# Two-layer ViT tower: the first expert layer's results are added by the scatter DMA in DRAM instead of on VectorE

## The reference

```
h = tok(x)                                        # patches, layer norm, product with W
h = h + quantised_attention(layernorm(h))         # layer 0
h = h + experts_of_4(layernorm(h))                # layer 0: each token goes to ONE of 4 experts (192 -> 768 -> 192)
h = h + linear_attention(layernorm(h))            # layer 1
h = h + experts_of_8(layernorm(h))                # layer 1: each token goes to TWO of 8 experts, weighted sum
```

## Time and profile before

| what | us |
|---|---|
| three runs: median (lowest to highest) | 627.05 (625.25 to 629.93) |
| the profiled execution's own time | 627.9 |
| its span, first to last instruction | 626.1 |
| busy in the span: PE / DVE / ACT / POOL | 503.8 / 326.7 / 206.9 / 143.4 |
| mean granted TensorE clock, share of full | 0.867 |

### The profile page before, as it was taken

One profiled execution on the slowest core, in us unless ns is written; L12 is line 12 of the kernel. 1 busy time (PEld: TensorE's weight loads), 2 busy tenths in 40 slices (PEclk: granted clock), 3 DMA queues, 4 the chain that ended last, 5 costly groups with the idle time before them and its releaser, 6 DMA issues.

```text
span 626.1 us, 12431 instructions
## 1 busy us (share of the span) xinstructions
PE 503.8 (80%) x4338; PEld 462.8 (74%) x4339; DVE 326.7 (52%) x1046; ACT 206.9 (33%) x439; POOL 143.4 (23%) x148
## 2 busy tenths in 40 slices
PE   4999999886543593799999599916999999999960
PEld 4999995465432493689999485915899999999950
DVE  1668999678998786122221464794222222222207
ACT  4620034666993164034343151250222111221110
POOL 1590000000001000533421100004344544343220
PEclk9999999899556575699999787856999999999995
DMA  9981000000004002965669400025866665567116
GB/s 321 409 317 22 1 1 1 1 3 1 0 2 177 2 0 102 227 202 161 187 187 369 136 2 0 1 101 163 243 182 184 201 201 166 162 186 200 55 54 273
DMA packets 35379, 81.41 MB, mean 130 GB/s; under 512 B 7142, under 2 KB 18242, under 8 KB 34306
## 3 DMA queue, kind: packets, MB, share of 16 engines
q1 hardware_dynamic: 29762, 69.37, 33.9%
q0 software_dynamic: 5568, 11.41, 6.5%
HBM read 70.33 MB, written 10.42 MB: 129 GB/s over the span
## 4 chain that ended last, share of the span: by engine, by line
PE 69%; DVE 15%; ACT 6%; DMA 4%; issue 3%; SPq 2%; ACTq 0%; POOL 0%; DVEq 0%; POOLq 0%
PE ps L1088 18%; PE ps L847 14%; PE ps L1064 12%; PE ps L1072 6%; DVE h L1855 2%; PE ps L828 2%; PE ps L827 2%; DMA arena<-ffn_b 2%; PE ps L787 1%; PE ps L959 1%; PE ps L931 1%; DVE xT L1699 1%; PE ps L812 1%; PE ps L932 1%; DVE arena L1567 1%
## 5 line engine op out<-in xcount | busy, mean ns | idle before, releaser
L1088 PE MATMUL ps<-arena,xn 128*128 x696 | 123.3, 328 | 4.1 <-ACT xn L737 1.8
L1088 PEld LDWEIGHTS ps<-arena,xn 128*128 128x128 f32 x696 | 111.8, 190 | 6.6 <-issue 6.4
L481 POOL DMA_INDIRECT xT<-rows,from_i x58 | 56.0, 966 | 189.7 <-DVE from_i L1713 132.7
L1064 PE MATMUL ps<-xn,arena 128*128 128x128 f32 x696 | 91.6, 283 | 3.0 <-DMA arena<-ffn_b 2.0
L847 PE MATMUL ps<-arena 128*128 128x192 f32 (+1 forms) x588 | 86.3, 339 | 9.0 <-ACT arena L520 9.0
L1064 PEld LDWEIGHTS ps<-xn,arena 128*128 128x128 f32 x696 | 88.4, 199 | 4.8 <-DMA arena<-ffn_b 3.1
L847 PEld LDWEIGHTS ps<-arena 128*128 128x128 f32 (+1 forms) x588 | 84.8, 199 | 9.2 <-ACT arena L520 8.7
L494 POOL DMA_INDIRECT made<-xT,to_i x58 | 57.0, 983 | 110.6 <-DVE xT L1750 65.0
L1738 DVE COPY xn<-ps 128x128 f32<-128x128 f32 x58 | 16.9, 292 | 123.6 <-PE ps L1056 104.7
L740 ACT ACTIVATE xn<-ps 128x384 f32<-128x384 f32 x78 | 32.6, 493 | 126.2 <-PE ps L1074 100.1
L737 ACT ACTIVATE xn<-ps,b_all 128x128 f32<-128x128 f32 x114 | 30.9, 389 | 46.8 <-PE ps L1074 35.3
(11 more groups left out here) (368 smaller groups left out, 798.3 us busy)
## 6 DMA issues: line engine op xcount, KB each, us to landing
arena<-ffn_a SPq DMA_DIRECT2D x58, 384.0 KB
arena<-ffn_b SPq DMA_DIRECT2D x116, 96.0 KB
arena<-x_blocks SPq DMA_DIRECT2D x16, 384.0 KB, 6.8
arena<-x_strips SPq DMA_DIRECT2D x3, 1536.0 KB, 12.2
arena<-ffn SPq DMA_DIRECT2D x4, 1152.0 KB, 10.6
rows<-xn SPq DMA_DIRECT2D x8, 384.0 KB, 2.3
arena<-made SPq DMA_DIRECT2D x4, 768.0 KB, 6.7
arena<-tok_w SPq DMA_DIRECT2D x8, 288.0 KB, 7.1
```

The costliest lines, as they stand in the source:

```text
L481: pool.indirect_dma_start(sx[:, k % 6], None, F["src"], bass.IndirectOffsetOnAxis(from_i[:, k:k + 1], 0)).then_inc(sem(f"sx_in{k % 6}"), 16)
L1064: pe.matmul(ps[:, up_bank(u, c // 3), 128 * (c % 3):128 * (c % 3) + 128], w_up[:, u, 128 * c:128 * c + 128], sT[:, u, 0:128], start=(c % 3 ...
L1088: mm = pe.matmul(ps[:, result_bank(k, N), 0:DIM], hT[:, u % 2, 128 * c:128 * c + 128], F["w2"][:, bass.ds(e2 + DIM * c, DIM)], start=(c == ...
```

## The change

The semaphore counts of `h_row` fall by 4 behind the bridge, as the adds no longer raise it. F1's scatters stay plain copies (`ALU.bypass`).

```diff
-        got = [xn[:], view(0, [2 * NTOK, DIM])]
+        got = [h[:], view(0, [2 * NTOK, DIM])]
...
             sp.dma_start(gate_w1[1][0:K1], gate1_w[128:DIM, :]).then_inc(sem("gate_in"), 16)
+            sp.wait_ge(sem("cst_in"), 16)
+            sp.dma_start(made0[TOKS:TOKS + 128 * TILES0, :].rearrange("(k p) c -> p k c", p=128),
+                         cst[:, C_ID:C_ID + DIM].unsqueeze(1).to_broadcast([128, TILES0, DIM])).then_inc(sem("made_set"), 16)
...
             sp.dma_start(b2_all, ffn0_b2.to_broadcast([128, E0 * DIM])).then_inc(sem("b2_in"), 16)
+            for c in range(2):
+                sp.wait_ge(sem("h_row"), c + 1)
+                sp.dma_start(made0[0:TOKS, :].rearrange("(b t) c -> b t c", t=NTOK)[:, 8 * c:8 * c + 8, :],
+                             h[:, 8 * c:8 * c + 8, :]).then_inc(sem("made_set"), 16)
...
                 pool.wait_ge(sem("places"), 2 * n + 2)
+                if n == 0:
+                    pool.wait_ge(sem("made_set"), 48)
...
                     pool.indirect_dma_start(F["made"], bass.IndirectOffsetOnAxis(to_i[:, k:k + 1], 0), yo[:, k % 3],
-                                            None).then_inc(sem(f"y_st{n}{k % 3}"), 16)
+                                            None, compute_op=(ALU.add, ALU.bypass)[n]).then_inc(sem(f"y_st{n}{k % 3}"), 16)
...
             for i in range(4):
-                turn_rows(2, i, 3 + i)
+                pe.wait_ge(sem(f"back_{i}"), 16)
+                turn_rows(2, i, 2)
...
             for i in range(4):
                 dve.wait_ge(sem(f"back_{i}"), 16)
-                hs = h[:, 4 * i:4 * i + 4, :].rearrange("p a b -> p (a b)")
-                dve.tensor_tensor(hs, hs, xnf[:, 768 * i:768 * i + 768], ALU.add).then_inc(sem("h_row"), 1)
-            for i in range(4):
-                dve.wait_ge(sem("h_row"), 3 + i)
                 ins = ln_stats(4 * i, 4 * i + 4)
```

More of the change, by code:

```diff
@@ L1189, in out_products @@
                     if t >= 6 and t % 2 == 0:
-                        pe.wait_ge(sem("h_row"), 6 + t // 2 - 2)
+                        pe.wait_ge(sem("h_row"), 2 + t // 2 - 2)
                     mm = pe.matmul(lin_ps(t), PT[:, 128 * t:128 * t + 128], Bo, start=True, stop=True)
@@ L1196, in _ @@
             out_products(1)
-            turn_rows(3, 0, 8)
+            turn_rows(3, 0, 4)
             out_products(2)
             pe.wait_ge(sem("lin_p"), 4)
-            turn_rows(3, 1, 10)
+            turn_rows(3, 1, 6)
             logits(F1, 0)
             out_products(3)
-            turn_rows(3, 2, 12)
+            turn_rows(3, 2, 8)
             logits(F1, 1)
-            turn_rows(3, 3, 14)
+            turn_rows(3, 3, 10)
             logits(F1, 2)
@@ L1843, in _ @@
                 if b:
-                    dve.wait_ge(sem("h_row"), 6 + b)
+                    dve.wait_ge(sem("h_row"), 2 + b)
                     ln_stats(2 * b - 2, 2 * b)
-            dve.wait_ge(sem("h_row"), 14)
+            dve.wait_ge(sem("h_row"), 10)
             layer_norms(ln_stats(14, 16))
```

## The result

| | us |
|---|---|
| before, 22 runs: median (lowest to highest) | 624.78 (620.44 to 630.59) |
| changed, 22 runs: median (lowest to highest) | 621.19 (617.28 to 625.05) |
| ratio, with its 95% interval | 0.9942 (0.9921 to 0.9962) |
| the profiled execution: time, span, mean TensorE clock | 621.2, 619.4, 0.875 |

The change gains 0.6%, 3.6 us; the prediction had no change to speak of (+0.4 us) and a range whose lower end, 623.0, lies above the measured time.

The account below looks back on a forecast made before the run. TensorE bounds it, busy 504 of 626 us; in the bridge its arm ends 0.66 us after VectorE's. 627.9 - 1.0 + 1.3 + 0 = 628.2, with that execution 0.85 above the median: 627.4; range 623.0 to 633.5.

Parts of the forecast that it names:

- The adds, TensorE's arm: 1.0 us: Bridge between the layers: turning h waits for the first readback instead of the first add, gaining 1.0 us.
- VectorE's gain is hidden by the fillers: Bridge: VectorE gains 3.66 us but waits 3.3 us, as TensorE's 48 fillers run until L1151 at 368.6.
- the 2.7 it gives: Bridge, before L1151: fewer fillers would bring up to 2.7 us more of the removed VectorE work into the chain.
- The last landing: +1.3, ends 0 and 4.6: Layer 0's last scatter: accumulating makes it land 1.3 us later, paid once in the chain; bounds 0 and 4.6.
- the 0.8 worked out beside the sum: Last scatter: estimate from the Trainium skill's pages, landing about 0.8 us later, making the sum 0.5 us lower.
- a side remark: Expert loop: if GpSimd's 0.99 us per scatter doubled, it would still fit a tile; the last is inside the 1.3.
- Hidden in the loop, DMA room, fill and h writes: 0: Expert loop and before: longer landings, extra DMA work, the padding-row fill and two early h writes cost 0.
- "I take no net effect" of the clock: Half-clock stretches 353.3 to 363.3 and 373.7 to 383.9 us: no net effect from changed idle times, bounds -5 to +3.
- the clock keeps up: Rival, 0.11: shorter wait before turning h restores 2.4 GHz earlier, or no second low stretch behind L1151; 622.4.
- its second place: Rival's (0.11) other option: the pause behind L1151 no longer costs a second half-clock stretch.
- The readback's 5.13 us: Bridge: readback from issue to first landing, 5.13 us in the chain before, kept unchanged in the forecast.

Follow-up runs that it names:

- the two runs that isolate it: Changed kernel with plain F0 scatters: 0.9947 (0.9903 to 0.9990); kernel before with F0 scatters accumulating onto zeros, adds kept: 1.0038 (0.9986 to 1.0089).
- with the waits: Kernel before with 128 already fulfilled waits at the start of TensorE's program: 0.9950, then 0.9986 when repeated; changed kernel with the same waits: 0.9954.

## Why the prediction was wrong

- *The adds, TensorE's arm: 1.0 us.* Right. With no packet on either side, the first turn of h came 4.3 and 4.9 us after the readback's issue with the adds and 3.4 to 3.6 without: 1.1 us.
- *VectorE's gain is hidden by the fillers.* Right: VectorE ready 1.5 us early (3.3 were forecast, at the old pace of the turning; so fewer fillers were worth up to 3.3 by the prediction's own times, not the 2.7 it gives), and 14 fillers fewer took 1.5 us out of their row.
- *The last landing: +1.3, ends 0 and 4.6.* Right in size: +1.15 here, +1.1 and +1.2 in the two runs that isolate it; the 0.8 worked out beside the sum was too little. Half of it is GpSimd's own time, which the prediction let grow only in a side remark. The page "Collectives: The Full Stack" of the Trainium skill (section on the bandwidth ceiling) has a second source read as the cost of a reducing transfer; here the software queue's share grew from 6.5 to 8.1% for 19 accumulating scatters of 116 transfers. That is (0.081 x 619.4 - 0.065 x 626.1) / 19 = 0.5 us more of each engine for one, 0.85 in place of 0.35 (0.95 in place of 0.30 for the last one alone). That is 2.4 to 3 times the plain one, more than one doubled read would give.
- *Hidden in the loop, DMA room, fill and h writes: 0.* Right: TensorE's 17.74 of 18 us are unchanged, and both h writes landed 3.2 us after issue.
- *"I take no net effect" of the clock.* This step failed. The prediction kept TensorE's idle time during the readback as it was. But the last scatter lands later, the clock has fallen by then, and 16 fillers at half clock take 3.5 us in place of 2.5, while the wait is 1 us shorter by the add: the gap that was 3.6 us is closed, and 2.4 GHz is back before or during the turning. Part of this is chance: with accumulating scatters the 16 fillers took 3.3 to 3.7 us in every profile, with plain ones anything from 2.0 to 3.7, depending on when the clock fell. That is 1.2 us in the turning with the packet out of both (5.8 and 5.9 against 4.3, 5.2 and 4.6), 1.9 in the first pair of profiles. The prediction's rival "the clock keeps up" had the place and the first half of the reason, at 0.11; its second place, the stretch behind L1151, did not change in the first pair of profiles (10.2 us in both).
- *The readback's 5.13 us were taken as a property of the transfer.* This failed too, and it is the larger part: about 2 us hang on whether a packet of instructions falls into it, which the new code happens not to have. No row quoted ahead of the change could have shown it; the queue's own row in that stretch would have shown the packet, though not its price. That the packet lies outside in the changed kernel is luck and no merit of the edit as far as is known.

By these, +1.2 for the landing, -1.1 for the add and -1.2 for the clock make -1.1 of the change's own in the bridge (-1.0 measured), and the packet another -2.2 (20.3 to 18.1). Together that is -3.2 in the bridge (20.3 to 17.1, the means of two and three profiles), and it lies within the -3.6 of the time (-2.4 to -4.9). The split is shown in the profiles only. What is left open: the 17 profiles, whose work behind the bridge is the same but for a few fillers, differ there by up to 6 us (252 to 258 from L1151 to the end) with the places of the half-clock stretches, and whether the change shifts their mean was not settled. Also open is what sets the packet's place. TensorE's waits moved it, but two kernels that have the changed kernel's TensorE program up to the readback, the one without adds and the one with 34 late fillers, have it inside.

## What to carry to other kernels

Look at the instruction queue in the stretch of a short, exposed transfer before taking its landing as fixed; if a packet lies in it, a gain or a loss of 2 us in that stretch may belong to where the code lies and not to the edit, and a run with padding instructions, profiled more than once, can tell which. Removing work from one arm also changes how long the other engine idles, so re-reckon the clock and not only the waits. An accumulating scatter is cheap where its landing is hidden: here 19 of them cost 1.2 us in the chain, once.

## What was not expected of the hardware

- One 16 KB packet of instructions inside a readback of 1.5 MB delayed its first 384 KB piece from 3.2 to 3.8 us (nine profiles without one) to 4.4 to 6.0 (eight with one). In the kernel before the transfer ends with 1.2 us at 15 to 23 GB/s, about a sixteenth of the 385 GB/s at its height; with the waits, and no packet, nothing moves any more from 358.0 us on. So it seems that one engine of 16 lags and each piece waits for it; no row shows the single engines.
- GpSimd spends 1.58 us on issuing an accumulating scatter of 128 rows, 0.98 on a plain one, and the engines move the same 0.10 MB in 144 packets in place of 48.
- Stretches at half clock around the bridge lasted 3.4 to 13.7 us in these profiles. The clock fell both after idle times and while TensorE did products of 16 columns without a gap.
